# One read of 1024 columns between two scans, in place of two reads of 512 behind them

## What is computed

```python
def step(h, inp):
    u_t, d_t, B_t, C_t = inp
    dA = jnp.exp(d_t[..., None] * A)
    h = dA * h + (d_t * u_t)[..., None] * B_t[:, None, :]
    y = jnp.einsum('bdn,bn->bd', h, C_t)
    return (h, y)
...
xr = run_bidir(xr, rp)      # along the rows
xc = run_bidir(xc, cp)      # along the columns
x_rec = 0.5 * (xr + xc)
```

## Time and profile before

| | |
|---|---|
| median of three runs | 30124.23 us |
| the profiled execution, its own time | 30110.14 us |
| its span | 30108.4 us |
| VectorE busy | 26587.2 us |
| GpSimd busy | 24961.9 us |
| PE matmul busy | 19403.3 us |
| ScalarE busy | 17086.1 us |

### The profile page before, as it was taken

How to read it: one execution, slowest core, us unless ns; L and a number is a source line. 1 busy time by engine, 2 the same in 40 slices (tenths; PEclk the granted TensorE clock), 3 DMA queues, 4 the chain that set the end, 5 groups by cost and what they waited for, 6 DMA issues and landing times. The chain is left out here.

```text
span 30108.4 us, 292058 instructions
## 1 busy us (share of the span) xinstructions
PE 19403.3 (64%) x60570; PEld 5912.7 (20%) x60570; DVE 26587.2 (88%) x29741; ACT 17086.1 (57%) x23361; POOL 24961.9 (83%) x10756
## 2 busy tenths in 40 slices
PE   6666666666666666666666666666666666652873
PEld 1111111111111111111111111111111111112321
DVE  8999999999999999999999999999999999983111
ACT  5666666666666666666666666666666666640031
POOL 8999999999999999999999999999999999970000
PEclk7777777777777777777777777777777777775886
DMA  4555555555555555555555555555555555567657
GB/s 176 185 184 186 185 186 186 186 186 186 186 186 186 186 186 186 185 185 190 195 197 196 193 195 197 196 191 197 195 193 194 197 196 191 197 184 152 131 104 170
DMA packets 1885490, 5556.59 MB, mean 185 GB/s; under 512 B 329944, under 2 KB 593896, under 8 KB 1855464
## 3 DMA queue, kind: packets, MB, share of 16 engines
q1 hardware_dynamic: 1884792, 5550.56, 54.6%
HBM read 4744.46 MB, written 805.31 MB: 184 GB/s over the span
## 5 line engine op out<-in xcount | busy, mean ns | idle before, releaser
L756 POOL TENSOR_TENSOR drive<-du_rep,b_rep 128x1024 f32<-128x1024 f32 x8192 | 19137.1, 2357 | 1973.7 <-DVE state L692 1132.2
L692 DVE TENSOR_TENSOR_SCAN decay<-decay,drive 128x512 f32<-128x512 f32 x11264 | 13146.6, 1212 | 894.3 <-issue 570.1
L568 ACT ACTIVATE decay<-delta_rep,a_neg 128x1016 f32<-128x1016 f32 x8192 | 9054.1, 1108 | 2539.8 <-DVE state L692 1867.9
L705 DVE TENSOR_TENSOR read<-decay,c_rep 128x512 f32<-128x512 f32 x11264 | 7142.2, 676 | 0.0
L765 POOL TENSOR_TENSOR read<-state,c_rep 128x1024 f32<-128x1024 f32 x2560 | 6045.2, 2361 | 1.7 <-DVE state L692 1.7
L692 DVE TENSOR_TENSOR_SCAN state<-decay,drive 128x512 f32<-128x512 f32 x5120 | 5960.5, 1206 | 0.0
L431 PE MATMUL y_bank<-read,sel_f 128*32 128x512 f32 x32768 | 4837.8, 717 | 141.8 <-POOL read L765 116.3
L408 PE MATMUL p_bank<-e_one,sel_f 128*128 128x512 f32 x2048 | 1795.6, 973 | 4282.1 <-DVE e_log L677 2314.9
L564 ACT COPY decay<-zeros 128x8 f32<-128x8 f32 x5632 | 934.9, 166 | 5153.7 <-DVE read L705 5142.1
L395 PE MATMUL p_bank<-u,to_dt 128*128 128x512 f32 x2048 | 2099.5, 1128 | 2304.6 <-ACT zs L613 1440.8
L385 PE MATMUL p_bank<-xt,taps 128*128 128x512 f32 x4096 | 2615.7, 771 | 387.7 <-ACT bc L525 384.5
(11 more groups left out here) (90 smaller groups left out, 14458.5 us busy)
## 6 DMA issues: line engine op xcount, KB each, us to landing
du_rep<-du_spread SPq DMA_DIRECT2D x2048, 512.0 KB, 6.2
delta_rep<-delta_spread SPq DMA_DIRECT2D x2048, 512.0 KB, 8.4
b_rep<-bc_spread SPq DMA_DIRECT2D x2048, 512.0 KB, 8.2
c_rep<-bc_spread SPq DMA_DIRECT2D x2048, 512.0 KB, 7.6
du_spread<-e_log SPq DMA_DIRECT2D x512, 512.0 KB, 2.7
delta_spread<-e_one SPq DMA_DIRECT2D x512, 512.0 KB, 3.6
xt<-in_xs SPq DMA_DIRECT2D x1024, 128.0 KB, 3.4
bc_spread<-bc SPq DMA_DIRECT2D x1024, 64.0 KB, 2.2
```

Source lines behind the costliest of these rows:

```text
L568: nc.scalar.activation(inner(place[:, :]), inner(delta_rep[:, j, :]), ACT.Exp, scale=a_neg[s][:, ROW * j + m:ROW * j + m + 1]).then_inc(s_ ...
L692: nc.vector.tensor_tensor_scan(out[:, px(d)][:, ::step], decay[PLACE[h][q]][:, px(d)][:, ::step], drive[:, q % DRIVE_RING, px(d)][:, ::ste ...
L705: nc.vector.tensor_tensor(read[:, q % READ_RING, px(d)], states[:, px(d)], c_rep[:, m, px(d)], ALU.mult).then_inc(s_read_v, 1)
L756: nc.gpsimd.tensor_tensor(drive[:, q % DRIVE_RING, :], du_rep[h][:, j, :], b_rep[:, m, :], ALU.mult).then_inc(s_drive, 1)
```

## The change

For each of VectorE's eleven pairs in a unit, the two reads of 512 columns become one of 1024. It stands between the forward and the backward scan of the next pair; that of pair 15 stands behind its own scans. The read waits once, for both scans of its pair. The semaphore `s_read_v` counts once a pair instead of twice, and those who wait for it ask for half the count.

```diff
@@ sum_row @@
-                pe.wait_ge(s_read_v, 2 * NV * U + 2 * vector_before(ROW * m + ROW))
+                pe.wait_ge(s_read_v, NV * U + vector_before(ROW * m + ROW))
@@ make_decay @@
-                    at_least(act, s_read_v, 2 * NV * (U - back) + 2 * vector_before(n) + 2)
+                    at_least(act, s_read_v, NV * (U - back) + vector_before(n) + 1)
@@ vector @@
-            def scan(U, h, q):
-                dve.wait_ge(s_decay, PAIRS * U + q + 1)
-                dve.wait_ge(s_drive, PAIRS * U + q + 1)
+            def scan(U, h, q, d):
+                if d == FWD:
+                    dve.wait_ge(s_decay, PAIRS * U + q + 1)
+                    dve.wait_ge(s_drive, PAIRS * U + q + 1)
...
-                for d in range(2):
-                    step = 1 if d == FWD else -1
-                    nc.vector.tensor_tensor_scan(out[:, px(d)][:, ::step],
...
+                step = 1 if d == FWD else -1
+                nc.vector.tensor_tensor_scan(out[:, px(d)][:, ::step],
...
             def read_state(U, h, q):
...
-                for d in range(2):
-                    dve.wait_ge(s_state, 2 * PAIRS * U + 2 * q + d + 1)
-                    nc.vector.tensor_tensor(read[:, q % READ_RING, px(d)], states[:, px(d)],
-                                            c_rep[:, m, px(d)], ALU.mult).then_inc(s_read_v, 1)
+                dve.wait_ge(s_state, 2 * PAIRS * U + 2 * q + 2)
+                nc.vector.tensor_tensor(read[:, q % READ_RING, :], decay[PLACE[h][q]][:, :],
+                                        c_rep[:, m, :], ALU.mult).then_inc(s_read_v, 1)
...
                     for q in range(PAIRS):
-                        scan(U, h, q)
-                        if q not in BY_POOL:
+                        scan(U, h, q, FWD)
+                        if q > 0 and q - 1 not in BY_POOL:
+                            read_state(U, h, q - 1)
+                        scan(U, h, q, REV)
+                        if q == PAIRS - 1:
                             read_state(U, h, q)
```

More of the change, by code:

```diff
@@ L198, in scan_stage @@
         s_state = sem("state_halves")
-        s_read_v = sem("read_halves_by_vector")
+        s_read_v = sem("read_by_vector")
         s_read_g = sem("read_by_gpsimd")
@@ L689, in scan @@
                     out = decay[PLACE[h][q]][:, :]
-                for d in range(2):
-                    step = 1 if d == FWD else -1
-                    nc.vector.tensor_tensor_scan(out[:, px(d)][:, ::step],
-                                                 decay[PLACE[h][q]][:, px(d)][:, ::step],
-                                                 drive[:, q % DRIVE_RING, px(d)][:, ::step], 0.0,
-                                                 ALU.mult, ALU.add).then_inc(s_state, 1)
+                step = 1 if d == FWD else -1
+                nc.vector.tensor_tensor_scan(out[:, px(d)][:, ::step],
+                                             decay[PLACE[h][q]][:, px(d)][:, ::step],
+                                             drive[:, q % DRIVE_RING, px(d)][:, ::step], 0.0,
+                                             ALU.mult, ALU.add).then_inc(s_state, 1)
             def read_state(U, h, q):
                 m, j = group_of(q)
-                states = decay[PLACE[h][q]]
                 dve.wait_ge(s_c[m], 16 * (U + 1))
                 at_least(dve, s_ysum, ROW * U + m - 1)
-                for d in range(2):
-                    dve.wait_ge(s_state, 2 * PAIRS * U + 2 * q + d + 1)
-                    nc.vector.tensor_tensor(read[:, q % READ_RING, px(d)], states[:, px(d)],
-                                            c_rep[:, m, px(d)], ALU.mult).then_inc(s_read_v, 1)
+                dve.wait_ge(s_state, 2 * PAIRS * U + 2 * q + 2)
+                nc.vector.tensor_tensor(read[:, q % READ_RING, :], decay[PLACE[h][q]][:, :],
+                                        c_rep[:, m, :], ALU.mult).then_inc(s_read_v, 1)
             def gate(U, h, z_taken, projected):
```

## The result

The changed kernel takes 29457.92 us (median of four runs, 29453.22 to 29461.29) against 30122.55 us: ratio 0.9779, 95% interval 0.9762 to 0.9796. The forecast was 29575 with a range of 29250 to 29850.

A forecast was written before the change was run, and what follows sets the result against it. VectorE's own work (50.66 us a unit) bounds the kernel, plus the row set's code-loading stall and the column set's decay wait. Row set 618 us less, column set 68 more: 30110.1 becomes 29560, plus 14 gives 29575; range 29,250 to 29,850.

The forecast's parts named there:

- The stall goes because the loop's code is shorter: VectorE's loop over tiles, row set: 222 instructions for 266, so the 5 us pause at the branch back goes.
- The 618 us of the row set: Row set of the scan stage: 250 units fall from 53.87 to 51.40 us each, 618 us less.
- rival 2: VectorE's loop in the row set: the stall stays; chance 9%.
- A read of 1024 takes 1.124 us, 0.056 less than two: VectorE's eleven reads a unit: merging two of 512 saves 0.056 us each, bounds 0 to 0.08, 0.62 us a unit.
- VectorE's own work: Scan stage: a unit bound by VectorE alone falls from 50.66 to 50.05 us.
- Pair 3's read goes behind the gate and makes the gate wait: VectorE at the gate: the moved read makes a waiting unit 51.76 us against 51.25, 0.5 us longer.
- TensorE's row sum still ends 38.13 us behind the du product of pair 7: TensorE's sum ahead of the gate: its end stays 38.13 us after that product, so the gate can't start earlier.
- the waiting unit: Units in which VectorE waits: 175 of 258, 51.76 us in the unit laid out, 51.69 on average.
- The gate's wait: VectorE at the gate: waits for the row sum or "issue", about 1.3 us a unit, some 600 us in all.
- Pair 1's wait: First scan of pair 1: waits about 0.5 us for its decay, at no cost since pair 2 waits anyway.
- The column set loses 68 us: Column set of the scan stage: 260 units rise from 51.14 to 51.40 us, 68 us more.
- The row set becomes what the column set is: Scan stage: with the stall gone, gates come 51.4 us apart in both sets.

The follow-up runs named there:

- (1): Kernel before, plus 16 waits on a long past semaphore (8 instructions as built) ahead of VectorE's first loop: 29393.71 us, ratio 0.9766.
- (3): Kernel before, plus 64 waits on a long past semaphore (32 instructions as built) ahead of VectorE's first loop: 30012.38 us, ratio 0.9968.
- (4): Changed kernel, its VectorE code filled up with past waits ahead of each read to the kernel before's lengths: 30035.47 us, ratio 0.9972 to the kernel before.
- (7): Changed kernel with each read again two operations of 512, still between the next pair's scans, one wait for both: 29490.46 us, ratio 0.9793 to the kernel before.
- experiment 5: Changed kernel with its reads of 1024 left behind their own pair's scans: 29663.02 us, ratio 0.9855 to the kernel before.
- (6): Changed kernel with pair 3's read put back behind pair 3's scans, ahead of the gate: 29331.63 us, ratio 0.9744 to the kernel before.
- (8): Changed kernel with SyncE's last two delta loads issued ahead of the wait for row 2's sum and its c load: 29455.12 us, ratio 0.9782 to the kernel before.

## Why the prediction was right, and where it was not

*The stall goes because the loop's code is shorter.* Right, and shown from both sides: by a shift alone (1), by moving it to the other set (3), by filling the loop up again (4), and by a shorter loop at the old place (7). The packets of the instruction queue are 660 before, 35 after, and 660 in (3) and (4). The 618 us of the row set rest on the stall going (rival 2 is that it stays), and the forecast took that from the loop's 222 instructions and from a limit on the length that was the author's estimate. No run shows such a limit. What they show in its place: behind 187 instructions a loop of 266 stalls (the kernel before and experiment 4) and one of 244 doesn't (experiment 7), and the changed kernel's 222 behind 165 don't. A place alone can be enough too: behind 195 instructions a loop of 266 runs without the stall (1).

In the iteration of the earlier trace rows the packets start at 5558.8, 5565.3, 5567.9, 5570.3 and 5619.6, and the branch back at 5561.1; VectorE's next instruction is at 5567.1. One packet therefore comes 2.3 us ahead of the branch, and four behind it; the two pauses of the earlier trace rows end 2.0 and 1.7 us after the first two of these four start. A packet has 8.2 KB (5.41 MB over 660). What it holds no row tells, and why an iteration has five of them is not shown.

*A read of 1024 takes 1.124 us, 0.056 less than two.* Right where the read stands between scans (1.11 to 1.12 in the rows). Missing was what it costs behind its own pair's scan, 0.12 us more, which the changed kernel pays once a unit, for pair 15, and experiment 5 eleven times. VectorE's own work is 50.1 us by the shortest units of the changed kernel's trace (gates at 15658.70 and 15708.79), for the forecast's 50.05.

*Pair 3's read goes behind the gate and makes the gate wait.* Right in place and kind: it waits 427 times in the whole stage, and putting the read back (6) or removing the other candidate (8) shows which of the two sets the pace. The size was off, and this is the term that was mis-sized: "TensorE's row sum still ends 38.13 us behind the du product of pair 7". It ended at 37.39. TensorE's additions began 0.2 us sooner (29.36 behind the du product, 29.57 before) and took 6.11 us where they took 6.64: the third and fourth pairs of matmuls took 1.76 and 1.02 us, where they took 1.92 and 1.44. These are single units; over the column set's units in the two traces the row sum's end has medians of 37.93 (38.01 where pair 2 waited) and 37.39, so some 0.1 to 0.2 of the 0.74 lies in the choice of the unit in the earlier trace rows. From row sum to gate are 0.27 us, not 0.07, and gate to du product is 13.54 for the forecast's 13.56. So the waiting unit is 51.20 and not 51.76, and it is now nearly every unit, not two in three at 51.69 and one at 50.8: a mean of 51.20 for the forecast's 51.40. Two errors partly cancel in that mean, and this is luck: the waiting units come out 0.49 us shorter than forecast and the others 0.4 longer, so with 0.68 and 0.32 of them the mean falls by 0.33 and rises by 0.13. The 0.20 us between the two means is, over 510 units, 102 us of the 117 us between forecast and measurement. The gate's wait was forecast at 600 us and is 265: the row sum comes sooner, and pair 1's scan (120 us) and pair 2's (87 us) still take a part of VectorE's lead ahead of it. Pair 1's wait was forecast in place, at about 0.5 us; it is 0.25 us on average (118.3 us in 464 waits).

*The column set loses 68 us.* It lost some 16, from the same term.

*The row set becomes what the column set is.* Right: 51.20 both.

## What to carry to other kernels

Count the instructions of an engine's loop as built, and look for packets of the instruction queue in each iteration: here a body of 266 that started behind 187 instructions cost 5.3 us at each return (2 x 2.67), and eight idle instructions ahead of the loop saved 2.3%. A change that shortens code can be paid by that alone; test it by filling the code up again before giving the gain to the arithmetic.

Before moving work past an operation that waits for another engine, measure that wait's margin. The gate had 0.6 us, and 1.1 us of work moved behind it came back in part as a wait. A read of 1024 right behind its own pair's scans starts 0.12 us later here; split it, or put one other instruction between.

## What the runs showed that I had not expected

The pace of the changed kernel is very even. The tile view of experiment 8's gates, 145 to 13050 and 13700 to 26100:

```profile
L713 DVE TENSOR_TENSOR gated<-y_bank,zs x252: 690/692/693, 193.7 to 13044.8; 128x512 f32<-128x512 f32 x126
...
L713 DVE TENSOR_TENSOR gated<-y_bank,zs x242: 690/692/693, 13710.4 to 26049.6; 128x512 f32<-128x512 f32 x121
```

They are 12851.1 us apart over 251 units and 12339.2 us over 241, 51.20 us both, and single units lie between 51.19 and 51.21; in the kernel before they scatter between 50.66 and some 53 us in the column set. Why a cycle of three engines and a load queue settles on one value was not tried. It is part of what is open in the 0.74 us by which TensorE's row sum came sooner: with the regular pace the faster matmuls (1.92 us for a row sum that takes 3.64 us elsewhere) may always have fallen on the same work, and no run here separates cause from effect.

The stall costs less in the column set (53.51 us a unit in experiment 3) than in the row set (53.87 in the kernel before), with pauses that also fall on reads (130.9 us). That difference was not followed.
